# Graph attention and a hyperbolic mean on one core: loads in another order, x1 in two places, X_hi on ScalarE, a scalar chain in one piece

## The reference

```python
h = relu(layernorm(x))
mask = graph_id[:, None] == graph_id[None, :]        # 32 graphs of 64 rows in the first 2048 rows; the rest is one graph
q, k, v = h @ Wq.T + bq, h @ Wk.T + bk, h @ Wv.T + bv
scores = (where(mask, q @ k.T / 16, 0) + adj + adj) * where(mask, 1, -1e6)
x1 = x + (softmax(scores) * mask) @ v
h = relu(layernorm(x1))
XW = mobius_matvec(W, h)                             # tanh(|hW|/|h| * artanh(|h|)) * hW/|hW|
gamma = 2 / (1 - |XW|^2)
mean = (adj @ (gamma * XW)) / (adj @ (gamma - 1)), halved in the ball and scaled by the row sums of adj
out = x1 + expmap0(relu(logmap0(mean)))
```

## Time and profile before

| | us |
|---|---|
| runs | 828.32, 827.80, 822.64 (median 827.8) |
| profiled execution | 827.69 |
| its span, first to last instruction | 825.4 |
| TensorE, VectorE, ScalarE, GpSimd busy | 751.5, 641.6, 475.3, 112.0 |

### The profile page before, as it was taken

How to read it: one execution, slowest core, us unless ns; L and a number is a source line. 1 busy time by engine, 2 the same in 40 slices (tenths; PEclk the granted TensorE clock), 3 DMA queues, 4 the chain that set the end, 5 groups by cost and what they waited for, 6 DMA issues and landing times.

```text
span 825.4 us, 14748 instructions
## 1 busy us (share of the span) xinstructions
PE 751.5 (91%) x4989; PEld 690.2 (84%) x4996; DVE 641.6 (78%) x1231; ACT 475.3 (58%) x860; POOL 112.0 (14%) x228
## 2 busy tenths in 40 slices
PE   4999979999999998989596899999999999999980
PEld 4888767788888887867586799999999999999980
DVE  6768577777777777778578698888888888888874
ACT  2444276777777787757352465544555555545853
POOL 0000112211111221158022000000000000000080
PEclk9999989999999999999798989999999999999996
DMA  5115186877766876767912869999888898899641
GB/s 141 52 52 230 48 326 236 280 261 283 294 237 237 262 271 227 262 223 173 225 38 47 195 140 191 206 215 194 192 191 189 191 192 191 190 198 190 142 150 59
DMA packets 53288, 157.26 MB, mean 191 GB/s; under 512 B 8944, under 2 KB 30704, under 8 KB 47088
## 3 DMA queue, kind: packets, MB, share of 16 engines
q1 hardware_dynamic: 52688, 156.07, 69.9%
q10 hardware_dynamic: 544, 0.53, 0.2%
HBM read 148.16 MB, written 8.42 MB: 190 GB/s over the span
## 4 chain that ended last, share of the span: by engine, by line
PE 62%; DVE 16%; DMA 8%; ACT 5%; issue 4%; DVEq 3%; SPq 1%; ACTq 0%
PE bank L686 47%; PE bank L832 7%; DMA adjU<-in_adj 4%; DVE least L1695 4%; DVE adjT_lo L1501 3%; PE bank L752 2%; PE bank L818 2%; DMA x_scratch<-x 2%; ACT adjT_hi L1019 2%; DVE least L1682 1%; DMA adjL<-in_adj 1%; DVE bank L1493 1%; PE bank L678 1%; DVE X_lo L1481 1%; DVE turned L1493 1%
## 5 line engine op out<-in xcount | busy, mean ns | idle before, releaser
L686 PE MATMUL bank<-X_hi,adjT_hi 128*128 128x258 f32 x1024 | 293.1, 286 | 16.7 <-DVE adjT_lo L1501 16.6
L686 PE MATMUL bank<-X_lo,adjT_hi 128*128 128x258 f32 x1024 | 291.9, 285 | 0.0
L686 PE MATMUL bank<-X_hi,adjT_lo 128*128 128x258 f32 x1024 | 291.5, 285 | 0.0
L686 PEld LDWEIGHTS bank<-X_hi,adjT_hi 128*128 128x128 f32 x1024 | 195.6, 191 | 19.9 <-DVE adjT_lo L1501 16.1
L686 PEld LDWEIGHTS bank<-X_lo,adjT_hi 128*128 128x128 f32 x1024 | 196.0, 191 | 0.0
L686 PEld LDWEIGHTS bank<-X_hi,adjT_lo 128*128 128x128 f32 x1024 | 195.8, 191 | 0.0
L832 PE MATMUL bank<-values,probT 128*128 128x256 f32 x512 | 120.9, 380 | 1.4 <-ACT probT L1130 1.4
L1019 ACT CAST adjT_hi<-turned 128x1024 fp32r<-128x1024 f32 x64 | 67.1, 1048 | 78.9 <-PE bank L686 63.2
L1019 ACT CAST adjT_hi<-bank 128x1024 fp32r<-128x1024 f32 x64 | 64.8, 1013 | 73.1 <-PE bank L686 50.2
L832 PEld LDWEIGHTS bank<-values,probT 128*128 128x128 f32 x512 | 93.0, 189 | 14.6 <-ACT probT L1130 2.6
L1501 DVE TENSOR_TENSOR adjT_lo<-bank,adjT_hi 128x1024 fp32r<-128x1024 f32 x64 | 77.5, 1210 | 21.3 <-ACT adjT_hi L1019 21.1
(11 more groups left out here) (191 smaller groups left out, 1133.0 us busy)
## 6 DMA issues: line engine op xcount, KB each, us to landing
adjL<-in_adj SPq DMA_DIRECT2D x120, 512.0 KB, 8.6
adjU<-in_adj SPq DMA_DIRECT2D x32, 1024.0 KB, 6.2
adjL<-in_adj SPq DMA_DIRECT2D x16, 2048.0 KB, 10.4
xin<-in_x SPq DMA_DIRECT2D x8, 512.0 KB, 4.0
xt<-in_x SPq DMA_DIRECT2D x16, 256.0 KB, 4.1
adj<-in_adj SPq DMA_DIRECT2D x8, 512.0 KB, 9.2
x_all<-x_scratch SPq DMA_DIRECT2D x16, 256.0 KB, 10.7
out_x<-res SPq DMA_DIRECT2D x8, 512.0 KB, 3.3
```

Of the source, the lines that this page charges most:

```text
L686: last = pe.matmul(dst, a[i][a_cols], b[j][b_cols], start=(k_first and n == 0), stop=(k_last and n == 2))
```

## The change

1. SP's step: adjL of s+1 first, then the window, then the rest of adjU, then the x rows of s, then (in even steps from 4 on) the norms of pair s/2 - 2, and last the x1 store of s-2. After the steps: tile 1, norms, tile 2, tile 3, and only then the last two x1 stores, now by SP and not by ACT.
2. x1 has two places by the step's parity, each with a semaphore for its store; `attend` waits for the store of two steps before. The last two steps' norms are both copied by VectorE from x1 (`norms_beside`), the norms of pair 7 are not read back.
3. POOL forms the factor in `far_part` and sets the block by memset; two small tiles go.
4. X_hi of batch 1 is made by ACT (`points_high`), between its high parts. `point_roots` is split into `norm_roots` (two square roots, issued before the last `product_out`) and `product_roots`.
5. `points_factor` is cut into `points_kept` (3 operations), `points_length` (2), `points_conformal` (3) and `points_scale` (1), same operations; one product moves from ratio to argument. Batch 0's parts now stand ahead of score chunks 2 and 3 as well as at the step's end. For batch 1 norms, series, ratio and argument follow one another with no adj work between them; `adj_low(3)` and then kept, length, conformal and scale follow, and only then `first_turn(5)`.

```diff
-        x1 = place_small("x1", [P, 2, XW])
+        x1 = place_small("x1", [P, 2, 2, XW])
...
-        s_x1_out = sem("x1_stored")
+        s_x1_out = [sem("x1_stored0"), sem("x1_stored1")]
...
             def x1_store(s):
                 sp.wait_ge(s_csq, s.n + 1)
-                sp.dma_start(x1_halves[s.tile(HALFWAY)], x1[:, :, :]).then_inc(s_x1_out, 16)
+                sp.dma_start(x1_halves[s.tile(HALFWAY)], x1[:, s.par]).then_inc(s_x1_out[s.par], 16)
             def norms_back(m, stored):
-                sp.wait_ge(s_x1_out, 16 * stored)
+                for half in range(2):
+                    sp.wait_ge(s_x1_out[half], 16 * stored)
                 for a in range(QD):
                     norms_of(m, a, s_norms[1] if isinstance(m, int) and m >= BATCH_END[0] else s_norms[0])
...
                     if is_step(s, HT - 1):
                         sp.wait_ge(s_expL, HT - 1)
                         mean_adj(0, first_adj[0], d_adj[0])
-                    if not is_step(s, HT - 1):
+                    else:
+                        wait(sp, s_expL, s.n)
+                        sp.dma_start(adjL[:, nxt.par], adj_t[nxt.tile(HALFWAY)]).then_inc(s_adjL[nxt.par], 16)
                         sp.wait_ge(s_qk_used, (HC + 1) * s.n + HC)
                         sp.dma_start(adjU[:, HALF:N], adj_t[nxt.tile(HALFWAY) + HT][:, HALF:N]).then_inc(s_window, 16)
-                        wait(sp, s_expL, s.n)
-                        sp.dma_start(adjL[:, nxt.par], adj_t[nxt.tile(HALFWAY)]).then_inc(s_adjL[nxt.par], 16)
-                    if after(s, 1):
-                        x1_store(s.plus(-2))
-                    x_pair(s)
-                    if not is_step(s, HT - 1):
                         sp.wait_ge(s_expB, s.n + 1)
                         sp.sem_inc(s_sync_seen, 1)
                         sp.dma_start(adjU[:, 0:HALF], adj_t[nxt.tile(HALFWAY) + HT][:, 0:HALF]).then_inc(s_beside, 16)
-                    if s.par == 1 and after(s, 1) and not is_step(s, HT - 1):
-                        norms_back(s.plus(-3).m, s.n - 1)
+                    x_pair(s)
+                    if s.par == 0 and after(s, 3):
+                        norms_back(s.plus(-4).m, s.plus(-4).m + 1)
+                    if after(s, 1):
+                        x1_store(s.plus(-2))
                 steps(sp, step)
                 sp.wait_ge(s_expB, HT)
                 sp.wait_ge(s_qk_used, (HC + 1) * (HT - 1) + HC)
                 mean_adj(1, first_adj[1], d_adj_1)
-                norms_back(PAIRS - 2, HT - 2)
+                norms_back(PAIRS - 2, PAIRS - 1)
                 sp.wait_ge(s_expL, HT)
                 mean_adj(2, first_adj[2], d_adj[1])
-                sp.wait_ge(s_x1_last[0], 16)
-                for a in range(0, QD, 2):
-                    norms_of(PAIRS - 1, a, s_norms[1])
                 sp.wait_ge(s_qk, (HC + 1) * HT)
                 mean_adj(3, first_adj[3], d_adj_3)
-                sp.wait_ge(s_x1_last[1], 16)
+                x1_store(step_at(HT - 2))
+                x1_store(step_at(HT - 1))
+                for half in range(2):
+                    sp.wait_ge(s_x1_out[half], 16 * PAIRS)
...
-            def points_high(m):
-
-                pool.wait_ge(s_scale, 2)
-                for u in range(QD):
-                    t = u * PAIRS + m
-                    pool.tensor_scalar(X_hi[:, t, 0:D], product[:, t, 0:D], 0.0, v[8][:, t:t + 1], ALU.add,
-                                       ALU.mult).then_inc(s_hi, 1)
...
-                    pool.tensor_scalar(factor[:, :], same[:, s.par, :], 1.0 - FAR, FAR, ALU.mult, ALU.add)
-                    pool.drain()
                     wait(pool, s_maxL, s.n)
                     always(pool)
-                    pool.tensor_tensor(far_part[:, :], adjL_t[:, s.par, low, :], factor[:, :], ALU.mult)
+                    pool.tensor_scalar(far_part[:, :], same[:, s.par, :], 1.0 - FAR, FAR, ALU.mult, ALU.add)
                     pool.drain()
-                    pool.tensor_copy(adjL_t[:, s.par, low, :], pushed[:, :]).then_inc(s_pushed, 1)
+                    pool.tensor_tensor(far_part[:, :], adjL_t[:, s.par, low, :], far_part[:, :], ALU.mult)
+                    pool.drain()
+                    pool.memset(adjL_t[:, s.par, low, :], PUSHED_OUT).then_inc(s_pushed, 1)
...
-            def point_roots(batch):
+            def norm_roots(batch):
                 c = BATCH_COLS[batch]
-                act.wait_ge(s_msq, (2 * BATCH_END[batch]))
                 act.activation(quarters(roots[:, 0])[c], norms_slots[..., 0][c], ACT.Sqrt, bias=ln_eps[:, 0:1])
                 act.activation(quarters(roots[:, 1])[c], norms_slots[..., 1][c], ACT.Sqrt)
+
+            def product_roots(batch):
+                c = BATCH_COLS[batch]
+                act.wait_ge(s_msq, 2 * BATCH_END[batch])
                 act.activation(quarters(roots[:, 2])[c], msq_slots[c], ACT.Sqrt).then_inc(s_fa, 1)
+
+            def points_high(m):
+
+                for u in range(QD):
+                    t = u * PAIRS + m
+                    act.activation(X_hi[:, t, 0:D], product[:, t, 0:D], ACT.Copy, scale=v[8][:, t:t + 1]).then_inc(s_hi, 1)
...
-                point_roots(1)
+                product_roots(1)
                 adj_high(3)
                 point_logs(1)
                 adj_high(4)
+                point_tanh(1)
                 adj_high(5)
-                point_tanh(1)
-                for n in range(6, FIRST):
+                act.wait_ge(s_scale, 2)
+                points_high(4)
+                adj_high(6)
+                points_high(5)
+                adj_high(7)
+                adj_high(8)
+                points_high(6)
+                points_high(7)
+                for n in range(9, FIRST):
...
-                            x1_store(s.plus(-1))
...
-                x1_store(step_at(HT - 1))
                 cent_copy(step_at(HT - 1), 0)
                 adj_high(2)
                 product_out(step_at(HT - 3))
                 product_out(step_at(HT - 2), 6)
+                act.wait_ge(s_norms[1], 16 * QD * (PAIRS - 1 - BATCH_END[0]))
+                act.wait_ge(s_beside_norms, 2)
+                norm_roots(1)
                 product_out(step_at(HT - 1), 0)
-                act.wait_ge(s_norms[1], 16 * (QD * (PAIRS - BATCH_END[0]) - QD // 2))
-                act.wait_ge(s_beside_norms, 1)
                 mean_part()
...
-            def attend(groups, s, slot, b, stored=None):
+            def attend(groups, s, slot, b):
                 dve.wait_ge(s_pv, groups)
                 dve.wait_ge(s_xt[s.par], turns(s))
-                wait(dve, s_x1_out, 16 * s.n if stored is None else 16 * stored)
-                if stored is not None:
-                    dve.wait_ge(s_x1_last[0], 16)
-                dve.scalar_tensor_tensor(out=x1[:, slot, 0:D], in0=bank[b][:, 0:D], scalar=tot[:, slot:slot + 1],
+                wait(dve, s_x1_out[s.par], 16 * s.m)
+                dve.scalar_tensor_tensor(out=x1[:, s.par, slot, 0:D], in0=bank[b][:, 0:D], scalar=tot[:, slot:slot + 1],
                                          in1=xt[:, s.par, slot], op0=ALU.mult, op1=ALU.add).then_inc(s_x1, 1)
...
+            def points_series(batch, first=True, last=True):
                 v3, v6, v7 = (Vh[i][BATCH_COLS[batch]] for i in (3, 6, 7))
                 dve.drain()
-                tt(v6, v3, v3, ALU.mult)
-                dve.drain()
-                ts(v7, v6, 1.0 / 13, None, ALU.mult)
-                for c in (11, 9, 7, 5, 3):
-                    dve.drain()
-                    dve.scalar_tensor_tensor(out=v7, in0=v7, scalar=1.0 / c, in1=v6, op0=ALU.add, op1=ALU.mult)
-                dve.drain()
-                dve.scalar_tensor_tensor(out=v7, in0=v7, scalar=1.0, in1=v3, op0=ALU.add, op1=ALU.mult)
+                if first:
+                    tt(v6, v3, v3, ALU.mult)
+                    dve.drain()
+                    ts(v7, v6, 1.0 / 13, None, ALU.mult)
+                    dve.drain()
+                    dve.scalar_tensor_tensor(out=v7, in0=v7, scalar=1.0 / 11, in1=v6, op0=ALU.add, op1=ALU.mult)
+                    dve.drain()
+                if last:
+                    for c in (9, 7, 5, 3):
+                        dve.scalar_tensor_tensor(out=v7, in0=v7, scalar=1.0 / c, in1=v6, op0=ALU.add, op1=ALU.mult)
+                        dve.drain()
+                    dve.scalar_tensor_tensor(out=v7, in0=v7, scalar=1.0, in1=v3, op0=ALU.add, op1=ALU.mult)
...
                 first_turn(3)
                 adj_low(2)
                 first_turn(4)
-                dve.drain()
-                first_turn(5)
                 points_norms(1)
-                adj_low(3)
                 points_series(1)
-                adj_low(4)
                 points_ratio(1)
                 points_argument(1)
+                adj_low(3)
+                points_kept(1)
+                points_length(1)
+                points_conformal(1)
+                points_scale(1)
```

(45 more changed lines are left out.)

84 lines of the change are left out of this document (40 added, 44 removed).

## The result

The changed kernel takes **802.0 us** (median of 4 runs, 801.61 to 804.59) against 827.6 of the kernel before on the same chip (4 runs): ratio **0.971**, 95% interval 0.9666 to 0.9753. The profiled execution took 804.59, the longest of the four; its span is 802.8 us. The prediction was 805.0, range 797 to 818.

A forecast was written before the change was run, and what follows sets the result against it. TensorE was taken to bound attention, stand still before the mean, and VectorE to bound the mean's opening. Terms -8.5, -3.3, -8.95, -1.6 and -0.3 sum to -22.7, from 827.7 to 805.0 us; range 797 to 818.

The forecast's parts named there:

- steps, to the 14th window: Attention's steps: the rest of adjU leaves earlier, VectorE's wait goes, early points are cut up; -8.5 us.
- last step: Attention's last step, bound by GpSimd's chain: the scales come right after `centre`, so the chain starts earlier; -3.3 us.
- x1 in two places: Between attention and mean: the last `attend` awaits the store two steps back, so x1 forms at 393.7, not 402.63; -8.95 us.
- clock after the standstill: Last three products before the mean: without TensorE's standstill they no longer run at the lower clock; -1.6 us.
- opening: Opening of the mean, bound by VectorE: its ordered work from the roots to turn 10 shortens slightly; -0.3 us.
- table switch: Tanh's table before the joined chain: ready in time by the trace row, 1.28 us; by the page's 2.66, 806.3 us total.
- A: Attention's steps stay at 18.28 us from another cause; only the hole before the mean closes: 817 us, chance 0.18.
- D: Store two steps back is also late, steps gain nothing, only the clock's 1.6 us go: 826 us, chance 0.05.
- C: Attention's window lands only after adjL has ended, so a step lasts 20.5 us: 845 us, chance 0.05.
- B: Before the mean, tile 3 takes half of tile 2's bandwidth and the joined chain slips 6 us: 811 us, chance 0.08.

The follow-up runs named there:

- old_opening: Changed kernel with VectorE's and ACT's order in the mean's opening as before, the second scalar chain in two pieces, X_hi staying on ACT: 802.5 us.
- the wait put back: Changed kernel with the last attend waiting again for the x1 store of the step before, that store issued by ScalarE: 812.3 us.
- the last two kernels: Changed kernel with mean_scales ahead of chunk 15's low part: 797.2 us; that kernel with turns from chunk 8 one low part earlier, scales moved again: 790.4 us.

## Why the prediction was right, and where it was off

The terms, each against the trace (us):

| term | predicted | measured |
|---|---|---|
| steps, to the 14th window | -8.5 | 347.25 to 339.26: -8.0 |
| last step | -3.3 | -2.5 |
| x1 in two places | -8.95 | 402.63 to 393.74 in the run with this alone: -8.9 |
| clock after the standstill | -1.6 | cent to roots 9.8, was 11.5: -1.65 |
| opening | -0.3 | roots to end of turn 10, 31.35 to 30.4: -0.95 |
| sum | -22.7 | -22.0 at the piece, -22.6 in the span |

The last step's is the rest: x1 formed at 383.26 and not at 402.63 (-19.37), less the first and the third term. The first term is net of 0.4 us by which the profile of the changed kernel was behind at the second window (130.50 and 130.08).

- **Steps.** Mechanism right, in all its signs: no wait of `least` for adjU, the rest of adjU right behind its release, no wait for the window, plain steps of 17.4. The split was off by as much each way: the ten steps gave 7.4 and not 6.0, the two before them 1.0 and not 2.5. I let 2.7 us of early points stay in the ten steps; three steps of 18.55, 17.55 and 17.56 hold 1.4. From the second window to the fourth I took 31.4 us as TensorE's content, a full step less the product; TensorE is busy 16.30 and 16.20 us in those two steps, 32.5 in all, so at most 1.8 and not 2.9 was to be had. And the reason I gave for the small remainder in the steps, the cutting of the points, was wrong: whole points cost the steps nothing in the new order. They cost the last step instead.
- **Last step.** GpSimd's chain was the right bound, and TensorE waited for `own` (2.0 us). The chain itself gave more than the -3.3: `own` came 39.7 us after the fourteenth window and not 43.5, -3.75, and 1.9 of it go to the cut points. The shortfall of 0.8 behind it has a place: TensorE's last eight matmuls, right behind that wait, took 3.31 us, and 1.73 in the profiles of the old opening, of the wait put back and of the last two kernels, with the same wait in front of them.
- **x1.** The term came out at x1 itself, but the kernel with this part alone gained 5.2 at the piece, not 8.95 + 1.6: tile 2 was right behind. The prediction did say that tile 1 and tile 2 improve with the shortened last step; it didn't say that the term needs it. It took the median of tile 2's pieces, 14.7 us, for the landing of the tile, where the last piece took 17.7. Margins there are small even now: 1.26 us of wait for tile 2 and 1.23 for the roots.
- **Opening.** The run with GpSimd's X_hi shows +1.2 us at the piece, the run with the old chain 0.2 the other way. So the 0.95 comes from X_hi on ACT and not from the joined chain. On the table switch the row was right: Tanh's table was in and its result there at 401.1, before the chain asked at 402.7. The 2.66 us that the Trainium skill (ScalarE: Activation LUTs, What ACT_TABLE_LOAD costs) counts with a drain aren't seen: the load took 1.28 and the ACTIVATE began 0.02 us behind it.
- **The 3 us between forecast and median.** The forecast was made against one execution, and for that it was 0.4 us off (804.59). That execution had the lower clock where the three others, at 801.6 to 802.3, most likely had not: against the profile of old_opening, the same time by its runs, it lost 1.0 us before the window of step 0 (99.43 and 98.43), 0.6 more until the fourteenth, and 1.58 at the eight matmuls. The run with the window first shows the same pair of times, 804.56 and 804.34 against 801.88 and 801.84, and its profile, of an 804.56, has the eight matmuls at 3.27. Of the faster runs there is no trace, so this stays an inference.

**The rivals.** A (817, the steps stay) and D (826, the store two steps back is late) fell: steps of 17.4 us, no wait for the store. C (845, the window behind adjL late) fell: VectorE never waited for a window, and the two orders take the same time. B (811, tile 3 takes tile 2's bandwidth) fell twice: turn 4 waited 1.26 us for tile 2 and the chain didn't slip by 6, and holding tile 3 back gave tile 2 only 0.3 us. Tile 2 is the near bound all the same, most likely because it stands behind tile 1. The prediction's own figure for its pieces, a median of 14.7 us, was close (14.1).

## What to carry to other kernels

Put the load whose buffer is free ahead of one that waits for another engine, on every queue: the x1 store and x rows in front cost 0.7 us a step with whole points and 0.4 with cut ones. When a long wait closes, list what stands within a few microseconds behind it, with its landing time: x1's second place was worth 5.2 us alone and its full price only with tile 2 issued earlier, and the cut-up points saved 3.4 us in the steps in one load order, and nothing there but some 3 us in the last steps in the other. And look in a written-out order for `turn n, low n` where `turn n+1, low n` is possible, and for a small chain that another engine awaits behind work nobody needs yet: these two moves, without one instruction more, gave 11.6 us, nearly half of what the whole change gave.

## What was not expected of the hardware

- The same wait of 2.0 us was followed by matmuls at the lower of TensorE's two clock levels (1.2 and 2.4 GHz) in some executions and at the upper in others: eight took 3.23 to 3.31 us in four profiles and 1.73 in four. The mean granted clock from 376 to 384 was 0.79 in three of the first kind (in the fourth the matmuls began at 383.4) and 1.00 in the second. A difference of 1.6 us between two single profiles can be this alone.
- With two tiles of 2 MB in flight, the second sent 2 us behind the first, the last piece of the first landed 18.8 us after its issue, and 18.5 without the second. Only the later one paid, 22.9 us for a piece against 7.8. Two stores of 258 KB sent on ScalarE's queue beside a tile went with 19.6 us for its last piece, against 16.6 where they were sent behind it.
- The wait of 5.37 us before the long piece cost 1.5 us behind its end too: the granted clock was 0.50 for the first 2 us of the piece, and the piece lasted 269.34 us, against 267.81 behind a wait of 1.67.
